# Layer 0's feed-forward: conversion, moments and normalisation set one, two and three turns behind the product of gate and up, with the loop written out

## The reference, cut to what matters

```python
def _act_quant(x):
    scale = 127.0 / jnp.clip(jnp.max(jnp.abs(x), axis=-1, keepdims=True), 1e-05)
    xq = jnp.clip(jnp.round(x * scale), -128.0, 127.0) / scale
    return x + jax.lax.stop_gradient(xq - x)

def _bitlinear(x, w):
    return jnp.einsum('bsi,oi->bso', _act_quant(x), _weight_quant(w))

gate = jax.nn.silu(_bitlinear(x, w_gate))      # 256 -> 1024
up = _bitlinear(x, w_up)
return _bitlinear(gate * up, w_down)           # 1024 -> 256
...
x = _layernorm(x + _L0_ffn_ref(x, L0_ffn_w_gate, L0_ffn_w_up, L0_ffn_w_down), axis=-1)
```

## Time and profile before

| | |
|---|---|
| median of 3 runs | 2842.53 us (2834.94 to 2843.1) |
| the profiled execution's own time | 2841.1 us |
| its span, first to last instruction | 2839.2 us |
| mean granted clock of TensorE | 0.92 |
| busy: PE, PEld, DVE | 2413.6, 1898.3, 1404.6 us |
| busy: ACT, POOL | 870.9, 679.7 us |
| the stage's first row (the row maxima of X) | at 528.60 us |
| first row of TensorE in the next stage | at 659.71 us |

### The profile page before, as it was taken

The page is one execution under the profiler, slowest core; times in us unless marked ns, Lnnn a source line. Parts: engine busy times, 40 slices in busy tenths (PEclk is TensorE's granted clock), DMA queues, the critical chain, the costliest instruction groups (busy, mean ns, idle before and its releaser), DMA issues. The chain is left out here.

```text
span 2839.2 us, 53500 instructions
## 1 busy us (share of the span) xinstructions
PE 2413.6 (85%) x20565; PEld 1898.3 (67%) x20565; DVE 1404.6 (49%) x2851; ACT 870.9 (31%) x1510; POOL 679.7 (24%) x1006
## 2 busy tenths in 40 slices
PE   6969999667979899899979988956987879679993
PEld 3847777433568745699958866635846767479992
DVE  3246666576548731112147755752145888621114
ACT  1124333364324321011122224401334655212223
POOL 1932222231223300022211210112311222123332
PEclk9879999888989999999989999967988999889996
DMA  9020000100020000388810002003610000079994
GB/s 345 1 85 1 0 0 1 31 0 1 0 84 2 2 30 0 144 322 309 300 47 1 0 5 83 3 30 115 173 34 5 2 2 3 31 261 323 326 323 157
DMA packets 163568, 254.21 MB, mean 90 GB/s; under 512 B 17744, under 2 KB 124369, under 8 KB 163153
## 3 DMA queue, kind: packets, MB, share of 16 engines
q1 hardware_dynamic: 154192, 230.92, 23.7%
q0 software_dynamic: 9216, 21.06, 2.7%
HBM read 220.29 MB, written 31.13 MB: 89 GB/s over the span
## 5 line engine op out<-in xcount | busy, mean ns | idle before, releaser
L3212 PE MATMUL te_pU<-te_xsT,te_wu 128*128 128x128 f32 x1952 | 235.2, 278 | 1.7 <-DMA te_wg<-in_L_ffn_gate 1.0
L3212 PEld LDWEIGHTS te_pU<-te_xsT,te_wu 128*128 128x128 f32 x1952 | 232.7, 194 | 5.5 <-issue 2.5
L3233 PE MATMUL te_pY<-te_wd,te_hT 128*128 128x256 f32 x976 | 220.8, 379 | 0.0
L3233 PEld LDWEIGHTS te_pY<-te_wd,te_hT 128*128 128x128 f32 x976 | 180.7, 190 | 22.1
L1117 PE MATMUL x_pB<-early,x_xlT 128*128 128x384 f32 x384 | 139.5, 508 | 4.7 <-DVE x_qn L1344 3.0
L3253 ACT ACTIVATE te_hT<-te_pU 128x512 f32<-128x512 f32 x78 | 46.6, 597 | 242.5 <-PE te_pU L3212 242.5
L3271 DVE COPY te_ys<-te_pY 128x256 f32<-128x256 f32 x61 | 25.9, 424 | 162.8 <-PE te_pY L3233 162.8
L2279 DVE TENSOR_REDUCE x_mx<-x_pR 128x8 f32<-128x1024 f32 x64 | 78.3, 1223 | 53.0 <-PE x_pR L2063 51.2
L1117 PEld LDWEIGHTS x_pB<-early,x_xlT 128*128 128x128 f32 x384 | 71.9, 198 | 48.6 <-issue 6.9
L3266 DVE TENSOR_TENSOR te_hT<-te_pU,te_sg 128x512 f32<-128x512 f32 x44 | 30.4, 692 | 149.4 <-ACT te_sg L3251 149.4
L3251 ACT ACTIVATE te_sg<-te_pG 128x512 f32<-128x512 f32 x44 | 26.3, 597 | 251.4 <-PE te_pG L3212 251.4
(11 more groups left out here) (630 smaller groups left out, 5846.1 us busy)
## 6 DMA issues: line engine op xcount, KB each, us to landing
te_wu<-in_L_ffn_w_upT SPq DMA_DIRECT2D x39, 1024.0 KB, 5.7
te_wd<-in_L_ffn_w_downT SPq DMA_DIRECT2D x39, 1024.0 KB, 5.8
te_wu<-in_L_ffn_up SPq DMA_DIRECT2D x22, 1024.0 KB, 4.9
te_wg<-in_L_ffn_gate SPq DMA_DIRECT2D x22, 1024.0 KB, 7.0
te_wd<-in_L_ffn_down SPq DMA_DIRECT2D x22, 1024.0 KB, 7.8
moe_first<-in_L_ffn_W SPq DMA_DIRECT2D x8, 1024.0 KB, 8.6
xs_slots<-zeros SPq DMA_DIRECT2D x1, 5120.0 KB, 23.5
ys_slots<-zeros SPq DMA_DIRECT2D x1, 5120.0 KB, 35.5
```

What stands on the lines that cost most here:

```text
L3212: ins = pe.matmul(out[g][:, m, :], w[:, k, bass.ts(PER * g + m, P)], xsT[:, k, :], start=(k == 0), stop=(k == KD - 1))
L3233: ins = pe.matmul(pY[u][:, 0, :], hT[:, k, :], wd[u][:, k, :], start=(k == 0), stop=(k == KH - 1))
```

## The change

The hardware loop goes: each engine's program is written out over turns -2 to 19 (`TURNS`), with each part left out where its block doesn't exist (`live`). `since` waits for an event of block b, or for nothing where b is negative. h and hr get a second copy each. The order inside a turn n is new:

- VectorE: h of n, xn of n-3, reduction to sd of n, hq of n-1, moments of n-2.
- TensorE: G and U of n+1, pt of n+2, pX of n-3, pT and y of n-1.
- ScalarE: xr of n+2, gate of n+1, XT of n-3, xqT of n+2, hr of n, hqT of n-1.
- GpSimd: rstd and X of n-3, xres of n-2, xq of n+2.

Each instruction's work and shape stay. Cut to its core, the diff is:

```diff
-        gate, h, hr = s.sb("gate", [P, F]), s.sb("h", [P, F]), s.sb("hr", [P, F])
+        gate = s.sb("gate", [P, F])
+        h, hr = ([s.sb(f"{n}{i}", [P, F]) for i in range(2)] for n in ("h", "hr"))
...
+        TURNS = range(-2, NB + 4)
...
+            for n in TURNS:
+                if live(n - 3):
+                    tail.pool(pool, n - 3)
+                if live(n - 2):
+                    tail.pool_residual(pool, n - 2)
+                if live(n + 2):
                     inputs(n + 2)
...
+            for n in TURNS:
+                if live(n + 1):
+                    gate_and_up(n + 1)
+                if live(n + 2):
+                    input_transposes(n + 2)
+                if live(n - 3):
+                    tail.tensor(pe, n - 3)
+                if live(n - 1):
+                    down(n - 1)
...
+            def rounded(b):
+                since(act, inv_ready, b)
+                since(act, hq_ready, b - 2)
+                act.activation(hr[b % 2][:], h[b % 2][:], ACT.Identity, bias=magic[:], scale=inv2[:]).then_inc(hr_ready, 1)
...
+            for n in TURNS:
+                if live(n + 2):
                     rows(n + 2)
+                if live(n + 1):
                     gates(n + 1)
+                if live(n - 3):
+                    tail.scalar(act, n - 3)
+                if live(n + 2):
                     inputs(n + 2)
+                if live(n):
+                    rounded(n)
+                if live(n - 1):
+                    hidden(n - 1)
...
+            def products(b):
+                h_steps.turn(b)
+                since(dve, gate_ready, b)
+                since(dve, u_ready, b)
+                since(dve, hr_ready, b - 2)
...
-            skewed(dve, turn)
-            moments(NB - 1)
-            tail.normalize(dve, NB - 1)
+            for n in TURNS:
+                if live(n):
+                    products(n)
+                if live(n - 3):
+                    tail.normalize(dve, n - 3)
+                if live(n):
+                    scales(n)
+                if live(n - 1):
+                    integers(n - 1)
+                if live(n - 2):
+                    moments(n - 2)
```

More of the change, by code:

```diff
@@ L1527, in input_transposes, with gate_and_up @@
                 ins.then_inc(xqT_ready, 1)
[L1529 to L1532, removed]
+            def gate_and_up(b):
+                since(pe, xqT_stored, b)
+                since(pe, gate_ready, b - 1)
                 for w, out, ready in ((wgb, pG, g_ready), (wub, pU, u_ready)):
-                    if not first and out is pU:
-                        pe.wait_ge(h_ready, b)
+                    if out is pU:
+                        since(pe, h_ready, b - 1)
                     for n in range(N):
@@ L1541, in gate_and_up, with down @@
                     ins.then_inc(ready, 1)
[L1543 to L1550, removed]
+            def down(b):
+                since(pe, hq_ready, b)
+                since(pe, hqT_stored, b - 1)
                 for k in range(KF):
@@ L1585, in gates, with rows @@
[L1585 to L1593, removed]
-                    rows(n + 2)
[L1595 to L1599, removed]
+            def rows(b):
+                since(act, xq_ready, b - 1)
+                act.activation(xr[:], core.X[:, b, :], ACT.Identity, bias=magic[:], scale=inv[:, b:b + 1]
+                               ).then_inc(xr_ready, 1)
@@ L1600, in turn, with hidden @@
+            def hidden(b):
+                since(act, hqT_ready, b)
+                if b:
+                    act.wait_ge(tail.y_ready, b)
+                act.copy(hqT[:], pT[:]).then_inc(hqT_stored, 1)
+            act.wait_ge(magic_ready, 1)
+            for n in TURNS:
+                if live(n + 2):
+                    rows(n + 2)
+                if live(n + 1):
                     gates(n + 1)
-                if next2:
+                if live(n - 3):
+                    tail.scalar(act, n - 3)
+                if live(n + 2):
@@ L1602, in turn @@
                     inputs(n + 2)
[L1603 to L1616, removed]
@@ L1632, in moments, with integers @@
+            def integers(b):
+                since(dve, hqT_ready, b - 1)
+                since(dve, hr_ready, b)
+                dve.tensor_scalar(hq[:], hr[b % 2][:], MAGIC, 127.0, ALU.subtract, ALU.min).then_inc(hq_ready, 1)
             def moments(b):
                 t_steps.turn(b)
-                tail.sums(dve, t_steps, b, y[:], scale=sd[:, bass.ds(b, 1)])
+                tail.sums(dve, t_steps, b, y[:], scale=sd[:, b:b + 1])
                 t_steps.end()
[L1637 to L1660, removed]
```

69 lines of the change are left out of this document (31 added, 38 removed).

## The result

| | before | changed |
|---|---|---|
| median of this comparison's runs | 2840.51 us (4 runs) | 2826.49 us (4 runs, 2821.65 to 2829.09) |
| ratio, 95% interval | 1 | 0.9951 [0.9937, 0.9964] |
| profiled execution, its span | 2841.1, 2839.2 us | 2825.35, 2823.4 us |

The changed kernel is faster, by 14 us by this comparison's ratio (10 to 18). A second comparison, of the same kernel, gave 2829.07 us and a ratio of 0.9965 [0.9951, 0.9978]: 10 us. I had forecast 2836 and a range from 2829 to 2843: too small a gain, and a range that does not hold the first result. The forecast "within 0.3%" did not come either: it was 0.49% here and 0.35% in the second comparison.

What follows compares the result with a forecast made beforehand. VectorE's order alone was taken to set the 7.00 us turn. Gains of 1.1 + 6.3 + 1.1 - 2.1 = 6.4 us off 2841.1 gave 2834.7, so an expected median of 2836, range 2829 to 2843.

Steps and rivals of the forecast that it cites:

- The sum as a sum for the whole kernel: All the stage's terms summed to 6.4 us off the whole kernel, with no other stage changing.
- Steady part: From h of turn 3 to h of turn 15: 84.2 us before, 83.1 after, gain 1.1.
- the ring: New cycle through TensorE (3.10) and ScalarE (3.10): 6.2 us a turn at full clock, just above VectorE's 6.1.
- The clock as the price of the ring: In the steady part, 20.6 us of low TensorE clock costs 8.7 us, between 6.5 and 10.3.
- Filling: Turns 0, 1 and 2 hold less on VectorE: 13.4 us in place of 19.7, gain 6.3.
- Start: Stage start: table load runs beside G and U, h(0) waits for U and not for gate; gain 1.1.
- Draining: Stage end: hq(15) comes 6.6 to 7.3 us after its h; 15.5 us in place of 13.4, loss 2.1.
- Unrolling: Writing out the loop: 13 turns lose 0.53 us each, with no other VectorE wait to hide it in.
- Rival A: Clock never falls in the new cycle: steady part 74.4, gain 15, 2827 us; chance of a gain over 8.5: 0.23.
- Rival B: VectorE's hq meets GpSimd's xq: first case, hq waits, 2838; second, only xq held, absorbed, own sum; chance 0.12.
- Rival C: Low clock lasts, each turn 9.0 us, whole 18.5 us slower, 2861; chance slower at all 0.12, over 0.3% 0.06.
- Rival D: Nothing happens: another wait returns each turn's 0.5 us, draining costs what filling gives; 2841 us, chance 0.10.

Runs made afterwards that it cites:

- e4: Changed kernel with ScalarE's copy XT of n-3 moved to the end of the turn, behind hqT: 2812.83 us, ratio 0.9905 to before.
- e7: Changed kernel with XT last on ScalarE and eight extra 256-column matmuls in TensorE's idle time ahead of y: 2812.07 us, ratio 0.9906 to before.
- e3: Changed kernel with eight extra 256-column matmuls (the filler) in TensorE's idle time ahead of y: 2815.82 us, ratio 0.9921 to before.
- e6: Kernel before with eight extra 256-column matmuls (the filler) in TensorE's idle time ahead of y: 2835.78 us, ratio 0.9991 to before.
- e2: Kernel before with this stage's loop written out, its order unchanged: 2832.55 us, ratio 0.997 to before.
- e8: Kernel before, written out, with only xn and what follows it one turn later: 2853.35 us, ratio 1.0054 to before.
- e9: e8 with pX of n-2 moved on TensorE from behind y to ahead of pT: 2821.98 us, ratio 0.9922 to before.

## Why the prediction was right and wrong, point by point

**The sum as a sum for the whole kernel: wrong, and the step that failed.** The working ended in 6.4 us for the stage, and the stage gave 6.6 and 6.7 in two traces and 9.7 in one. Then it said "no other stage changes" and turned 6.4 us of a stage into 6.4 us of a median, with a range from the cases of the stage alone. That step failed: the term for everything outside the stage, put at nothing, came out at 3 to 7 us. Measured by ratios, the kernel gained 14 and 10 us; the spans outside the stage fell from 2707.8 and 2708.1 to 2701.0 to 2702.6. The stage's 9.7 alone would have given 2840.5 - 9.7 = 2830.8, inside the range. Of the 9.5 us between 2836 and 2826.5 some 4 are this term, 3.3 the stage's in that trace, and 2 the base, a median of before of 2840.5 where I had 2842.5. The parts outside by themselves vary by 7 to 8 us from one execution of a kernel to the next. The runs show that such a part exists in every comparison, and that it goes with the granted clock of stages that were not edited; what makes the clock differ there stays open. A range for a change of 6 us in a span of 2839 had to allow for it.

**Steady part: the mechanism right, two terms mis-sized.** The forecast gain of 1.1 became 3.5 in the first trace and 1.3 in the other two. VectorE's list is 5.54 (e4, e7), not 6.1, and below my lower bound of 5.95: beside rstd, the short waits for the reduction's input and for sd went too, as xn and hq now stand in those gaps (in the rows above xn and r stand without a wait for rstd or sd). The ring at the full clock is 5.97 from h to h, not 6.2: TensorE's part is 3.23 (3.10 forecast), ScalarE's 2.75 (XT at 596.40 to y at 599.15; 2.84 in the turn after it, whose hr starts 0.10 later; 3.10 forecast), since hr and hqT start 0.10 us before the row ahead of them ends, and y follows hqT after 0.06. 12 times 5.97 is 71.6, so the low clock cost 9.1 us in the first trace and 11.3 in the others, against 8.7 and a bound of 10.3; e3 bears this out directly with 10 to 12. In the first trace the two errors, 2.8 us too much for the ring and 0.4 too little for the clock, give the 2.4 us by which the gain was forecast too small; in the others they nearly cancel (2.8 against 2.6), which is luck.

**The clock as the price of the ring: right.** e3 and e6 are the proof: the same filler is worth 10 to 12 us after the change and nothing before it. The low clock covers 20.5 us of the first trace's steady part and 23.9 of the others' (clock 0.873 and 0.856), where I took 20.6, and each us of it cost 0.44 and 0.47, where I took 0.42. The ring that I called cold, with a 9.0 us turn, came only in part: the clock was back before U, so a fall cost 1.68 us (7.65 against 5.97), once in every second turn.

**Slips in the working.** An even spread of the low clock gives 0.31 x 20.6 = 6.4, not 6.5. B's 2838 is counted from 2841.1, where the other rivals are counted from 2842.5; from there it is 2839.4. The chances of the five cases add up to 1.04. The forecast hangs on none of these.

**Filling:** 6.3 forecast, 7.1, 6.1 and 6.1 measured. **Start:** 1.1 forecast, 1.2 to 1.3 measured, by the path named (h waits for U, not for gate). **Draining:** a loss of 2.1 forecast, 2.2 measured, with hq(15) at 6.62 us behind its h, in the 6.6 to 7.3 given. **Unrolling:** 0.53 a turn forecast, 0.56 measured (e2), but only in turns that the clock covers; "VectorE had no other wait to hide it in" left out that a low-clock turn needs some 7.0 us in that order as well.

**Rival A, the clock holds (0.23): its price, not its mechanism.** It gave 2827, and the median is 2826.5. That is luck: the clock in the steady part is 0.86 to 0.87, not 1.00. With the clock held (e3) the kernel takes 2815.8. The Trainium skill (TensorE: Matmul & The Clock Gate, "Why this matters for your kernels") would have had the clock stay up, since it ties a fall to a long idle gap. The gaps here were 2.4 us, shorter than the gap that this page of the Trainium skill names, and the clock fell in every second turn: this trace does not bear that rule out. The section "A second HAM failure mode: psum-queue depth-cycling" of the same page of the Trainium skill describes a clock that swings because the engine idles briefly between groups of matmuls; that is nearer to what the rows show. No run says what exactly decides: e4 kept 0.98 with gaps of 1.86 us, and before fell to 0.88 with gaps of 1.1.

**Rival B, hq meets xq: its second case came in each of the turns shown.** xq takes 1.60 us beside hq where it takes 1.07 alone, hq keeps its 0.69, and pt waits for U anyway: xq ends at 601.33, pt starts at 601.76. Absorbed, as said; and xq was held for 0.51 to 0.53 us, less than all of hq. rstd, no longer beside hq, takes 0.56 and not 0.96.

**Rival C, a cold ring: real, but not here.** A clock of 0.78 and turns of 7.7 to 9.1 came in e8, in which another wait closed the ring. **Rival D:** excluded by both intervals.

## What to carry to other kernels

When a lag moves waits off the busiest engine, write down the new ring engine by engine and take out of it whatever nobody on it needs: here one 0.37 us copy, moved to the end of ScalarE's turn, was worth more (11 to 15 us of the stage, 3.6 where the clock was held) than the whole change (7 to 10). A low TensorE clock cost next to nothing here while VectorE set the pace, and became the largest cost once TensorE was in the ring; matmuls put into its idle time tell which of the two it is. Before moving a step further back, look for who reads its output tile: a reader that stands behind the long products turns the lag into a wait, as in e8, and moving that reader turned a loss of 15 us into a gain of 22.

## What the runs showed of the hardware

A shorter turn does not keep the clock up by itself: 0.88 and 0.92 (before, 7.0 us turns), 0.87 (e2, 6.4 to 7.0), 0.87 (changed, 5.97 and 7.65), but 0.93 (e9, mostly 5.76) and 0.98 (e4, 5.5). Eight 256-column matmuls a turn in the gap, about 1.05 us, brought it to 1.00 in the changed kernel. And the traces of one kernel agree in their span to 0.14% (2823.4, 2827.2, 2825.5) while the part ahead of the stage, with the same code in all of them, differs by 8 us, with a granted clock of 0.93 where it is long and 0.94 to 0.95 where it is short: a few us in one part of one trace are no evidence for a change elsewhere.
